# Metaformer block on Trainium2: the routing sum of the mix stage in one burst per block

## The reference

```python
x = x + conv(ln(x), l_pair, protein_pair, inter_pair, ...)   # triangle products, gate, projection
t = tokens(x)                                                 # 36864 tokens of 128 channels
t = t + ffn(ln(t), Wr, br, W1, b1, W2, b2, gamma, beta)
# conv ends in:   g = sigmoid(zn @ Wend + bend);  out = g * (ln(block) @ Wsum + bsum) * zm
# ffn begins in:  logits = mean(ln(t), axis=tokens) @ Wr + br;  two experts of 8 are chosen for the one batch row
```

## Time and profile before

| | us |
|---|---|
| median of 3 runs | 1392.8 (1388.87 to 1396.92) |
| the profiled execution | 1393.41 |
| its span, first to last instruction | 1391.7 |
| TensorE busy | 1330.3 (96%) |
| VectorE busy | 1125.8 (81%) |
| ScalarE busy | 997.8 (72%) |
| GpSimd busy | 881.5 (63%) |

### The profile page before, as it was taken

One profiled execution on the slowest core, in us unless ns is written; L12 is line 12 of the kernel. 1 busy time (PEld: TensorE's weight loads), 2 busy tenths in 40 slices (PEclk: granted clock), 3 DMA queues, 4 the chain that ended last, 5 costly groups with the idle time before them and its releaser, 6 DMA issues. The chain is left out here.

```text
span 1391.7 us, 30986 instructions
## 1 busy us (share of the span) xinstructions
PE 1330.3 (96%) x9880; PEld 1131.8 (81%) x9880; DVE 1125.8 (81%) x3049; ACT 997.8 (72%) x2327; POOL 881.5 (63%) x1415
## 2 busy tenths in 40 slices
PE   6999999999999997999899999799999999999995
PEld 3887788877788777989667776699999999999994
DVE  6888887888778874778798887677888888888897
ACT  3988888988888886555477775346777667777773
POOL 3867768777677765444388887335555555555574
PEclk9999999999999998999999999799999999999998
DMA  9999999999999999888799994211222232222213
GB/s 215 245 259 256 260 251 256 270 264 268 236 242 262 262 249 305 276 276 290 193 316 325 318 319 151 96 32 61 77 77 80 73 92 77 77 76 77 79 59 91
DMA packets 357522, 267.41 MB, mean 192 GB/s; under 512 B 60433, under 2 KB 332723, under 8 KB 357363
## 3 DMA queue, kind: packets, MB, share of 16 engines
q1 hardware_dynamic: 355800, 264.76, 70.9%
q10 hardware_dynamic: 1290, 0.46, 0.2%
q0 software_dynamic: 272, 0.21, 0.1%
HBM read 171.02 MB, written 94.37 MB: 191 GB/s over the span
## 5 line engine op out<-in xcount | busy, mean ns | idle before, releaser
L1534 ACT ACTIVATE hT<-psH_d,b 128x512 f32<-128x512 f32 x288 | 197.9, 689 | 151.3 <-PE psH_d L1574 151.3
L595 POOL TENSOR_SCALAR shared<-shared,coefs_early 128x128 f32<-128x128 f32 x468 | 204.4, 456 | 89.7 <-DVE coefs_early L355 89.7
L652 PE MATMUL psZ_a<-w_all,xT_a 128*128 128x128 f32 x1728 | 230.1, 276 | 2.2 <-DVE ip_prod L732 1.8
L652 PE MATMUL psZ_a<-w_all,xT_block 128*128 128x384 f32 x576 | 213.9, 494 | 2.0 <-DVE ip_prod L732 2.0
L652 PEld LDWEIGHTS psZ_a<-w_all,xT_a 128*128 128x128 f32 x1728 | 209.8, 192 | 5.4 <-ACT xT_a L567 4.0
L583 ACT ACTIVATE sig_a<-psZ_a 128x256 f32<-128x256 f32 (+1 forms) x360 | 153.8, 427 | 70.3 <-PE psZ_a L652 44.8
L1228 DVE TENSOR_SCALAR shared<-shared,coef 128x128 f32<-128x128 f32 x288 | 185.5, 704 | 1.6 <-POOL xh_b L1608 1.6
L639 PE MATMUL psT_a<-ident,shared 128*128 128x128 f32 x1152 | 185.5, 273 | 1.0 <-DVE mask L262 1.0
L639 PEld LDWEIGHTS psT_a<-ident,shared 128*128 128x128 f32 x1152 | 142.8, 142 | 47.6 <-issue 27.4
L1601 POOL TENSOR_TENSOR u_d<-u_d,gamma 128x512 f32<-128x512 f32 x72 | 93.5, 1298 | 129.3 <-ACT u_d L1517 128.0
L96 DVE BATCH_NORM_STATS2 stats_early<-shared 128x6 f32<-128x256 f32 x336 | 126.8, 420 | 33.3 <-DMA shared<-L_conv_protein_pair_dram 16.9
(11 more groups left out here) (220 smaller groups left out, 2959.0 us busy)
## 6 DMA issues: line engine op xcount, KB each, us to landing
shared<-in_x_dram SPq DMA_DIRECT2D x48, 512.0 KB, 6.2
scratch_xT<-xT_block SPq DMA_DIRECT2D x36, 512.0 KB, 5.3
shared<-scratch_xT SPq DMA_DIRECT2D x36, 512.0 KB, 5.5
scratch_x<-x_c SPq DMA_DIRECT2D x36, 512.0 KB, 4.5
shared<-scratch_x SPq DMA_DIRECT2D x36, 512.0 KB, 3.6
shared<-in_x_dram SPq DMA_DIRECT2D x48, 256.0 KB, 5.4
shared<-L_conv_protein_pair_dram SPq DMA_DIRECT2D x24, 512.0 KB, 6.8
shared<-in_L_conv_l_pair_dram SPq DMA_DIRECT2D x24, 512.0 KB, 8.7
```

The costliest lines, as they stand in the source:

```text
L595: return nc.gpsimd.tensor_scalar(x, x, r, b, ALU.mult, ALU.add)
L652: ins = nc.tensor.matmul(out, turned_x(G, i, t0, size)[:, j * P:j * P + P], rhs[i], start=True, stop=True)
L1534: nc.scalar.activation(hT[:, S % 2, f, :], psH[:, f, :], ACT.Gelu, bias=s["b1"][:, f:f + 1]).then_inc(gelued, 1)
```

## The change

The routing sum of a block stands in slot 8 of the following block, all 24 tiles one after another, behind psW of that slot. It waits for coefs2_ready once and raises `routed` by 12 at its end. Tile t still goes to row 32 (t mod 4) of psR. The stage's TensorE queue now runs on for 9 slots after the last block, of which the ninth holds the routing of the last block, and VectorE's for 8.

```diff
-        ROUTE_FROM = 10
+        ROUTE_AT = 8
...
-                if j >= ROUTE_FROM:
-                    (rm, rpar), pair = last_block(m, par), j - ROUTE_FROM
-                else:
-                    (rm, rpar), pair = (m - 1, par), j + PAIRS - ROUTE_FROM
-                if there(rm, rpar):
-                    if pair == 0:
-                        pe.wait_ge(coefs2_ready, 2 * (2 * rm + rpar + 1))
-                    if pair % 2 == 1:
-                        ends = isinstance(rm, int) and 2 * rm + rpar == NBLK - 1 and pair == PAIRS - 1
-                        for k in range(4):
-                            t = 2 * pair - 2 + k
-                            ins = nc.tensor.matmul(s["psR"][32 * k:32 * k + 1, 0:CH], coef_2(rm, rpar, t), x2[:, rpar, t, :],
-                                                   start=False, stop=ends)
-                        ins.then_inc(routed, 2)
+                rm, rpar = last_block(m, par)
+                if j == ROUTE_AT and there(rm, rpar):
+                    pe.wait_ge(coefs2_ready, 2 * (2 * rm + rpar + 1))
+                    for t in range(TPB):
+                        ends = 2 * rm + rpar == NBLK - 1 and t >= TPB - 4
+                        ins = nc.tensor.matmul(s["psR"][32 * (t % 4):32 * (t % 4) + 1, 0:CH], coef_2(rm, rpar, t),
+                                               x2[:, rpar, t, :], start=False, stop=ends)
+                    ins.then_inc(routed, PAIRS)
...
-            all_pairs(slot, PAIRS + ROUTE_FROM)
+            all_pairs(slot, ROUTE_AT + 1)
...
-            all_pairs(slot, ROUTE_FROM)
+            all_pairs(slot, ROUTE_AT)
```

## The result

| | before | after |
|---|---|---|
| median of 6 runs each, us | 1391.14 | 1397.99 |
| lowest to highest | 1388.69 to 1396.92 | 1396.59 to 1401.0 |
| span of the profiled execution | 1391.7 | 1399.3 |

The ratio is 1.0048, 95% interval 1.003 to 1.0065: slower by 6.7 us, between 4.2 and 9.0. The median ratio is just within 0.5%, as forecast, though its interval reaches 0.65%. The interval leaves out 1: the loss is real, and larger than the +1.6 us of the sum.

A forecast was written before the change was run, and what follows sets the result against it. TensorE was taken as the bound in middle blocks, by a tenth, VectorE close behind. 1.84 + 0.48 - 0.60 - 0.30 + 0.20 = +1.6 us on 1393.4, less 0.6 for the median, gave 1394.5 us; range 1386 to 1402.

The forecast's parts named there:

- the sum: Whole kernel: the changes in blocks 1 to 11 and the clock loss behind them add up to +1.6 us.
- the mechanism: Middle blocks: TensorE's gain falls where VectorE and GpSimd set the pace, the burst where they could run fast; +0.23 us each.
- the tail: Behind the last block before the change: 24 tiles in a row, 26 ns per record, taken as the burst's price.
- The wait for coefs2_ready: TensorE, slot 8: costs nothing, since VectorE writes those coefficients in slot 6, before the burst begins at 1.61 us.
- the loop from y to psW: Slow slots: TensorE's transpose waits for GpSimd's tile, so psW comes 2.34 us after the y three slots earlier.
- 14.99: Length in us forecast for a middle block with the burst, against 14.76 before.
- +1.84: Blocks 2 to 9: 8 x 0.23 us longer in all.
- +0.48: Block 1: us added to its 14.51, as it gets five more groups.
- the last two blocks: Blocks 10 and 11: shorter by 0.60 and 0.30 us, with bounds 0 to -1.2 and 0 to -0.6.
- the clock behind the last block: Last burst: longer TensorE idle time may lower the clock; +0.2 us taken, +1.2 at worst, 0 at best.
- TensorE as the only bound: Rival for the blocks: TensorE's gain of 1.26 us per block counts in full; -11.5, so 1381 us; chance 0.13.
- The expensive burst: Rival for slot 8, blocks 1 to 11: 59 ns per record; +13.7, so 1406.5 us; chance 0.18.

The follow-up runs named there:

- experiment 1: Changed kernel with GpSimd normalising its tile four slots ahead in place of three: 1390.02 us, ratio 0.9971 to the kernel before.
- experiment 2: Changed kernel with the routing in two bursts of 12 tiles, in slot 8 and in slot 2 a block later: 1391.83 us, ratio 0.9981 to the kernel before.
- experiment 5: Kernel before the change, with GpSimd normalising four slots ahead: 1392.39 us, ratio 0.9991 to the kernel before.
- experiment 3: Changed kernel with 18 unused identity transposes on TensorE while it waits for the last coefficients: 1397.61 us, ratio 1.0022 to the kernel before.
- experiment 4: Changed kernel with routing, and GpSimd's wait for it, left out for all blocks but the last: 1383.42 us, ratio 0.992 to the kernel before.
- experiment 6: Changed kernel with the burst in slot 11 in place of slot 8: 1397.4 us, ratio 1.0041 to the kernel before.
- experiment 7: Changed kernel with two bursts of 12 tiles (slot 8, slot 4 a block later) and GpSimd four slots ahead: 1388.5 us, ratio 0.996 to the kernel before.

## Why the prediction was right, and where its sizes were off

**Right: the mechanism, and with it the sign and the range.** The burst is as cheap as the tail had shown (2.56 from psW to psW, as forecast), TensorE's gain falls where it can't be used, VectorE stands in one place at slot 9, and the blocks are longer. Experiments 1, 2 and 5 show that it is the lead that is missing: more lead, or half of the burst where VectorE is the slower one, and the loss is gone; with spread routing more lead gives nothing in the middle blocks. The sizes below all missed to the same side. The time lies within the stated range; that the ratio came out just under 0.5% is luck. The wait for coefs2_ready cost nothing, and the clock stayed at 1.00 in the middle blocks though TensorE idled.

**Off: the loop from y to psW.** It was taken as 2.34 us from one place. In most blocks of the changed kernel it is 2.40, and in block 3 it is 745.57 - 743.08 = 2.49: the transpose at 744.83 is followed by psZ after 0.22 and by psW after another 0.52, where the row of before had 0.14 and 0.45. It stands twice in a block, at slot 8 (psW at 1.27 after the y of slot 6, not 1.09) and at the next slot 0 (1.15 after slot 11, not 1.02). In block 3 that is the difference between 14.99 and 15.27; blocks 2, 4 and 6 take 15.11 to 15.16. Over blocks 2 to 9 the steps into slot 8 are 0.75 us and those into the next slot 0 1.35 us longer than forecast. The kernel before was read a little short as well: not all its blocks take 14.76, blocks 2 to 9 average 14.81. Together they cost +3.68 in place of +1.84. Block 1 cost +0.89 in place of +0.48; in both kernels it spends some 0.25 us more ahead of slot 2 than the middle block from which its 14.99 was taken.

**Off: the last two blocks.** The middle between the floor of TensorE and no gain was taken: -0.60 and -0.30. They gave -0.29 and -0.17. Their slots run near 1.02 on GpSimd and VectorE too, so the burst stands out there as well (2.56 at slot 9).

**Off: the clock behind the last block.** Taken at +0.2, with +1.2 as the worst. In the two profiles the burst did cost 1.21 more, but 0.6 of it came back in the following stage, which the sum had not considered. That the longer idle time did it is not shown: in experiment 5 the burst took 2.74 us after 3.16 us of idle time, in experiment 1 it took 2.17 after 4.57.

**Not explained by any of these:** with the measured terms the sum is +4.1 and 0.6, 4.7 us. The measured 6.7 has an interval from 4.2 to 9.0, which holds it; experiment 3, the same kernel but for its tail, measured 3.1, with an interval from 0.3 to 6.0. The cause of the rest stays open. In the profiles it lies ahead of block 1, where the executions differ among themselves. The prediction said that 0.5% can't be told from no change: with 6 runs of each it could, down to 0.3%.

**The rivals.** TensorE as the only bound falls by experiment 4: without any routing blocks still take 14.03. The expensive burst falls by 1.49 us in every block from 1 to 11.
## What to carry to other kernels

An engine's gain is worth what the slots in which it falls can use: sum the engines slot by slot, not over the block, and ask how far the engine that gathers its work into a burst is ahead when the burst begins. What sets this lead can be a third engine's place in its own queue, here GpSimd's one tile; moving it one slot ahead turned a loss of 0.5% into a gain of 0.3%. Batching small matmuls saves what each group costs beyond its records (six groups took TensorE 2.82 us, the one burst 1.56). In these runs the saving was kept only where a batch was hardly longer than the lead, or stood where the consumer is the slow one.

## What the runs showed of the hardware

The same burst of 48 records behind the last block took 1.53, 2.74 and 2.52 us after an idle time of 3.16 us (kernel before, experiments 5 and 6), 1.94 and 2.74 after 3.80 (experiments 2 and 7), 2.17, 2.74 and 2.74 after 4.57 (experiment 1, the changed kernel, experiment 4), and 1.49 in both runs with TensorE filled up to 2.62 and 1.70 us ahead of it. In all eight executions without the filling the granted clock fell to the 1.2 GHz level, but at different points, from 2.1 us ahead of the burst's start (the changed kernel) to 1.3 us behind it (the kernel before). So after the same idle time the burst may run at either level, and a kernel with the routing spread can have this loss as well (experiment 5). The first y of block 1 lay 10 us apart between profiles of kernels that are the same up to there or nearly so; that is more than the change under study, and a reason to compare stretches of a profile rather than spans.
